# An attention and ternary feed-forward layer: weight sums totalled by a matmul with ones, the first split tiles of x in four buffers, order tables remade

## The chip, the core and the metric

The kernel runs on one core of a Trainium2 chip. The core has five engines with in-order queues of their own: TensorE (PE: matmuls and, beside them, weight loads), VectorE (DVE), ScalarE (ACT), GpSimd (POOL) and SyncE (SP), which here issues every DMA. They meet only at semaphores. The metric is the device time of one execution in microseconds (us), lower is better. A time is the median of several executions; the profile is of one execution.

## What is computed

```python
# 8 x 256 tokens, width 512; 16 heads of 32, 64 features a head; FFN width 2048
h  = layernorm(x)
q, k, v = h @ Wq.T + bq, ctx @ Wk.T + bk, ctx @ Wv.T + bv      # split into heads
qf, kf  = relu(q @ Wqf.T), relu(k @ Wkf.T) * mask
kv = sum_n kf v ; out = (qf kv) / (qf sum_n kf + 1e-8)
x  = x + out @ Wo.T + bo
# feed-forward with ternary weights and 8-bit activations
wq(w)  = clip(round(w / s), -1, 1) * s,   s = mean(|w|) over the whole matrix
xq     = 8-bit rounding of layernorm(x), row by row
a  = up(xq) * relu(gate(xq))**2 ; a = a * rsqrt(mean(a*a) + eps) * g
x  = x + down(8-bit rounding of a)
```

What matters below is s: the mean absolute value of each of the three matrices (gate, up, down). It is a sum over all rows and columns, so over all 128 partitions of the chip's memory too, and it must be known on every partition before a single weight can be rounded.

## The kernel before

There are two blocks. `attention` does everything up to the residual sum and makes the ternary weights on the side; `ffn` then runs over 16 tiles of 128 tokens. The change lies in the first alone.

**Turns.** The 16 token tiles are four groups of four. The attention block first makes keys and values of group 0 and then runs four turns, 0 to 3. Turn o does, for group o: F (key features), Q (queries), S (keys times values), R (query features), N (numerators and denominators); beside them K and V (keys and values) of group o+1 and O (output projection) of group o-1; turn 3 has P, the output projection of its own group. A unit such as Q2 fills one of the eight banks of PSUM, ACT reads the bank and writes the high half in fp16 (L747), DVE writes the low half (L879), and the bank is free. Each product is three fp16 matmuls (high by high, high by low, low by high). K, V, Q and O units are 12 matmuls of 128x512.

**What sets the order.** Nothing is scheduled at run time. `TURNS` is the order of the units on PE, and ACT and DVE go through the same list. `ACT_AFTER` and `DVE_AFTER` say behind which unit a piece of side work stands on those engines; POOL's and SP's orders are written out as lists of calls. A piece that stands too early blocks its engine until its input is there.

**Side work on the way to Q.** For tile n, `normalise` on ACT (L767) writes the normalised tile in fp32, into `xn` or, for tiles 1 and 2, into `o32`. `x_tile` on POOL splits it into two fp16 halves in `xn2` (L629, L632), which has two buffers; SP then issues a transposing DMA into `xT` (`turn_x`, L492). All Q units of a group wait for all four tiles. The attention's output goes the same way by `o_tile` (L641, L644), `o2` and `turn_o` (L501) to the O units. POOL also splits the context (L597 to L609, waits for `load_context`), adds the output bias (`add_bias`, L617) and makes the low half of kv (`kv_low`, L650).

**Side work on the weights.** Each of the three matrices comes in 8 pieces of 128x1024. `weigh(m, n)` on ACT sums the absolute values of a piece along each partition into a column of `wsum` (L795; its elementwise output goes to `junk`). `total(m)` on POOL sums the 8 columns over the partitions (L656). `weight_scale(m)` on DVE reduces the 8 totals to one number and inverts it into `winv` (L980 to L983). `chunk(c)` on ACT then rounds a piece with it (L807, through `wst`, two buffers) and takes the sign (L810). Matrix m is weighed in turn m and chunked in turn m+1. Pieces are loaded by SP (`raw_chunk`), some of them twice or three times, since space is scarce; `raw_up_even(k)` waits until the piece of gate weights in its place is rounded.

**Second layernorm.** DVE's `st2`, `large2`, `scale2` and `quant2` (L1186 to L1221) are statistics and 8-bit rounding of the group of the turn before.

Of the kernel before, what the change touches and what calls it, by code (L numbers as in the profile page):

```python
# [23 lines left out]
P = 128  # L24
# [32 lines left out]
def units(text):  # L57
# [9 lines left out]
    units(  # L67
# [4 lines left out]
    units(  # L72
# [4 lines left out]
    units(  # L77
# [19 lines left out]
        ("N", 6): (("weigh", 6),),
        ("K", 3): (("weigh", 7),),
# [41 lines left out]
    {  # L140
        ("F", 6): (("chunk", 0),),
        ("R", 4): (("kvh",),),
        ("R", 7): (("chunk", 1),),
        ("N", 1): (("chunk", 2),),
        ("N", 5): (("chunk", 3), ("chunk", 4)),
        ("O", 2): (("chunk", 5),),
# [7 lines left out]
        ("Q", 1): (("stats1",),),  # L154
        ("R", 3): (("ln1",),),
        ("N", 3): (("wo",),),
        ("V", 2): (("winv",),),
    },
    {
        ("F", 3): (("stats1",),),  # L160
        ("O", 0): (("st2", 0),),
        ("R", 3): (("st2", 1), ("ln1",)),
        ("Q", 3): (("st2", 2),),
        ("V", 0): (("st2", 3),),
        ("V", 1): (("large2",),),
        ("N", 7): (("scale2",),),
        ("V", 3): (("quant2", 0), ("quant2", 1), ("winv",)),
    },
    {
        ("O", 2): (("stats1",),),  # L170
        ("S", 0): (("st2", 1),),
        ("S", 1): (("ln1",),),
        ("R", 0): (("st2", 2),),
        ("K", 0): (("st2", 0),),
        ("N", 2): (("st2", 3),),
        ("N", 3): (("large2",),),
        ("V", 3): (("scale2",), ("quant2", 0), ("quant2", 1), ("winv",)),
# [3 lines left out]
        ("N", 3): (("st2", 1),),  # L181
        ("O", 3): (("st2", 3),),
# [15 lines left out]
    "O": "output projection",  # L198
}
# [79 lines left out]
def attention(nc, ps, xs, tern, area, ln2, wmean, x, ctxT, maskT, wqT, wkT, wvT, woT, wqfT, wkfT,  # L279
              bqT, bkT, bv, bo, wffn, xqb, xqT, xqb_ok, xqT_in):  # L280

    with ExitStack() as ctx:  # L282
# [45 lines left out]
        wtot = sb("wtot", [P, NCH])  # L328
# [89 lines left out]
        def _(sp):  # L418
# [1171 lines left out]
```

## Time and profile before

| | us |
|---|---|
| median of 3 executions | 445.12 (444.97 to 446.99) |
| profiled execution | 443.17 |
| its span, first to last instruction | 441.4 |
| attention block in it (until the barrier at 254.1) | 254.1 |
| PE busy in the span | 386.7 (88%) |
| DVE, ACT, POOL busy | 350.0, 316.9, 221.5 |

The profiled execution is 1.77 us longer than its span and 1.95 us shorter than the median. Times in the rows below are microseconds from the first instruction. "Idle before" is the time for which the engine did nothing ahead of the instruction, with the instruction that released it; "issue" stands where the profile shows no releaser.

### The profile page before, as it was taken

The page shows a single profiled execution, that of the slowest core. Times are in us where ns is not written, and L with a number is a line of the kernel's source. Part 1 is how long each engine was busy: PE and PEld are TensorE (multiplying, and loading weights), DVE is VectorE, ACT ScalarE, POOL GpSimd, SP SyncE. Part 2 cuts the span into 40 slices and gives each one's busy share as a digit, 9 for nine tenths or more (in the row PEclk, how much of TensorE's full clock was granted, in tenths as well). Part 3 has the DMA queues.
Part 4 walks back from the last instruction along what each step waited for, and adds up shares of the span by engine and source line. Part 5 has one row for each costly group of instructions (what it writes and reads, how often), then busy time and mean ns, then how long its engine had stood idle before and what let it go on. Part 6 is the DMA issues. An engine that isn't in the chain of part 4 may idle for free. (4 is left out here: it accounts for less than half of the span.)

```text
span 441.4 us, 8195 instructions
## 1 busy us (share of the span) xinstructions
PE 386.7 (88%) x2864; PEld 186.5 (42%) x2880; DVE 350.0 (79%) x718; ACT 316.9 (72%) x446; POOL 221.5 (50%) x210
## 2 busy tenths in 40 slices
PE   3986999819999889998979799899999989999955
PEld 1443545404555454455535344344444434344422
DVE  4765887472879589969888948999999999898962
ACT  5494387635978579888569359797979696988860
POOL 1074839162558428654276445474646463654420
PEclk9996999978999999999999989999999999999979
DMA  7846934736324904367064431452434242533324
GB/s 252 254 132 187 413 141 81 137 53 209 137 71 135 210 1 120 47 213 174 1 191 89 81 107 36 55 115 63 104 70 98 63 106 59 109 84 86 81 62 120
DMA packets 90872, 52.38 MB, mean 119 GB/s; under 512 B 78800, under 2 KB 78800, under 8 KB 90704
## 3 DMA queue, kind: packets, MB, share of 16 engines
q1 hardware_dynamic: 90832, 51.86, 45.5%
q8 instruction: 23, 0.38, 0.4%
q14 instruction: 17, 0.14, 0.1%
HBM read 28.78 MB, written 4.19 MB: 75 GB/s over the span
## 5 line engine op out<-in xcount | busy, mean ns | idle before, releaser
L1347 POOL TENSOR_TENSOR actg<-acts,subln 128x512 f32<-128x512 f32 x64 | 84.6, 1334 | 78.3 <-DVE acts L1430 73.8
L1527 PE MATMUL ps<-tern,area 128*128 128x512 bf16 x503 | 113.9, 382 | 3.8 <-PEq L282 2.7
L1527 PEld LDWEIGHTS ps<-tern,area 128*128 128x128 bf16 x512 | 49.8, 98 | 65.8 <-issue 4.9
L1540 PE MATMUL ps<-tern,aqT 128*128 128x512 bf16 x249 | 59.8, 390 | 12.3 <-DMA aqT<-aq 11.9
L1036 PE MATMUL ps<-xT,wqh 128*128 128x512 f16 x128 | 40.9, 403 | 13.4 <-DMA xT<-xn 13.4
L1358 ACT ACTIVATE relu<-ps 128x512 f32<-128x512 f32 x64 | 37.3, 582 | 21.2 <-PE ps L1527 21.2
L747 ACT ACTIVATE qkTh<-ps,bqk 128x512 f16<-128x512 f32 x32 | 21.4, 682 | 38.6 <-PE ps L1036 35.7
L1430 DVE TENSOR_TENSOR acts<-relu,ps 128x512 f32<-128x512 f32 x64 | 42.3, 679 | 5.9 <-ACT relu L1362 3.8
L1540 PEld LDWEIGHTS ps<-tern,aqT 128*128 128x128 bf16 x256 | 25.0, 100 | 45.6 <-DMA aqT<-aq 13.1
L1036 PE MATMUL ps<-woh,oT 128*128 128x512 f16 x128 | 40.1, 379 | 3.2 <-DVE vl L879 1.7
L879 DVE SCALAR_TENSOR_TENSOR fl<-ps,fh 128x512 f16<-128x512 f32 x64 | 40.3, 681 | 3.0 <-ACT fh L747 2.9
L879 DVE SCALAR_TENSOR_TENSOR qkTl<-ps,bqk,qkTh 128x512 f16<-128x512 f32 x32 | 23.5, 746 | 23.9 <-ACT qkTh L747 23.5
L1362 ACT ACTIVATE relu<-relu 128x512 f32<-128x512 f32 x64 | 40.3, 630 | 2.0
L1435 DVE TENSOR_REDUCE amax<-actg 128x1 f32<-128x1024 f32 x32 | 38.8, 1211 | 0.6 <-POOL actg L1347 0.2
L1369 ACT ACTIVATE square<-acts 128x2048 bf16<-128x2048 f32 x16 | 30.4, 1902 | 10.2 <-DVE acts L1430 10.2
L747 ACT ACTIVATE fh<-ps 128x512 f16<-128x512 f32 x64 | 34.2, 604 | 4.6 <-PE ps L1084 3.3
L1386 ACT ACTIVATE actg<-actg,magic_up,qs 128x2048 f32<-128x2048 f32 (+1 forms) x17 | 33.6, 1981 | 1.0 <-DVE qs L1449 1.0
L629 POOL TENSOR_TENSOR xn<-xn,zero 128x512 f16<-128x512 f32 x14 | 14.5, 1038 | 36.3 <-ACT xn L767 36.3
L641 POOL TENSOR_TENSOR o<-o,zero 128x512 f16<-128x512 f32 x16 | 16.6, 1036 | 30.4 <-issue 20.6
L1036 PE MATMUL ps<-ctxh,wkh 128*128 128x512 f16 x64 | 25.2, 394 | 7.3 <-DVE ctxl L867 7.3
L807 ACT ACTIVATE wst<-tern,magic,winv 128x1024 f32<-128x1024 f32 x20 | 24.7, 1234 | 8.9 <-issue 8.9
L1468 DVE TENSOR_SCALAR aq<-actg 128x2048 bf16<-128x2048 f32 (+1 forms) x17 | 23.8, 1401 | 7.9 <-ACT actg L1386 7.2
(160 smaller groups left out, 888.5 us busy)
## 6 DMA issues: line engine op xcount, KB each, us to landing
tern<-in_wffn SPq DMA_DIRECT2D x24, 512.0 KB, 5.4
out<-res SPq DMA_DIRECT2D x16, 256.0 KB, 2.1
area<-in_ctxT SPq DMA_DIRECT2D x3, 1024.0 KB, 5.5
xs<-in_x SPq DMA_DIRECT2D x3, 1024.0 KB, 10.0
oT<-in_wkT SPq DMA_DIRECT2D x4, 256.0 KB, 5.6
area<-in_ctxT SPq DMA_DIRECT2D x4, 256.0 KB, 6.1
fh<-in_wvT SPq DMA_DIRECT2D x4, 256.0 KB, 6.8
xs<-in_x SPq DMA_DIRECT2D x4, 256.0 KB, 7.5
```

The costliest lines, as they stand in the source:

```text
L747: nc.scalar.activation(out, in_, func, **kw).then_inc(high[stage], 1)
L879: nc.vector.scalar_tensor_tensor(out=out, in0=in0, scalar=scalar, in1=in1, op0=op0, op1=ALU.subtract).then_inc(drained[stage], 1)
L1036: mm = nc.tensor.matmul(acc, a, b, start=first and n == 0, stop=last and n == len(pairs) - 1)
L1347: nc.gpsimd.tensor_tensor(actg[:, s % 2, q], acts[:, s % 2, q], subln[:, q], ALU.mult)\
L1358: nc.scalar.activation(relu[:, u % 2, :], gate_bank(u), ACT.Relu).then_inc(relu_ok, 1)
L1362: nc.scalar.activation(relu2[:, u % R2, :], relu[:, u % 2, :], ACT.Square).then_inc(relu2_ok, 1)
L1369: nc.scalar.activation(square[:, :], acts[:, s % 2, :], ACT.Square, accum_out=ssq[:, s:s + 1])\
L1386: nc.scalar.activation(part, part, ACT.Identity, bias=magic_up[:, :], scale=qs[:, s:s + 1])\
L1430: nc.vector.tensor_tensor(acts[:, s % 2, 512 * c:512 * c + 512], relu2[:, u % R2, :], up_bank(u), ALU.mult).then_inc(acts_ok, 1)
L1435: return nc.vector.tensor_reduce(amax[:, s, h:h + 1], actg[:, s % 2, HALF * h:HALF * h + HALF], AX_X, ALU.max, apply_absolute_value=True)
L1527: mm = nc.tensor.matmul(acc, xqT[:, s % XT, k, :], weights[k][:, 512 * c:512 * c + 512], start=(k == 0), stop=(k == KC - 1))
L1540: mm = nc.tensor.matmul(down_bank(s), aqT[:, s % 2, k, :], down_w[:, k, :], start=(k == 0), stop=(k == FK - 1))
```

## The change

The sum over partitions leaves POOL. A new unit W is put into the list of turns 0 to 2, one for each matrix: PE multiplies a 128x128 fp32 matrix of ones by the 8 columns of `wsum`, so that each partition of a PSUM bank holds all 8 totals, and DVE reduces them from there. With that `total`, `wtot` and POOL's three reductions go.

`junk` becomes a view of the second buffer of `wst`; `chunk` uses only the first, and waits for the sign of the piece before. `split_x` puts the halves of tiles 2 and 3 into `o2`, the output's buffers, which are unused so early, so the first four tiles have four buffers; `o_tile` waits in turn until tiles 2 and 3 have been transposed.

The tables `TURNS`, `ACT_AFTER`, `DVE_AFTER` and the lists of POOL and SP are written anew. The diff, cut:

```diff
@@ TURNS, turn 1
-        "F0 F1 F2 F3 F4 F5 O0 O1 F6 F7 Q0 Q1 S0 S1 "
-        "O2 R0 R1 R2 R3 S2 S3 Q2 Q3 O3 K0 R4 R5 R6 "
-        "R7 K1 V0 N0 N1 N2 N3 V1 N4 N5 K2 N6 N7 V2 "
-        "K3 V3 "),
+        "F0 F1 F2 F3 O0 F4 F5 O1 F6 F7 S0 S1 Q0 Q1 "
+        "Q2 O2 R0 R1 R2 R3 K0 V0 Q3 S2 S3 K1 R4 R5 "
+        "R6 R7 O3 K2 V1 N0 N1 N2 N3 N4 N5 V2 K3 V3 "
+        "N6 N7 W0 "),
@@ DVE_AFTER, end of turn 2
-        ("V", 3): (("scale2",), ("quant2", 0), ("quant2", 1), ("winv",)),
+        ("N", 2): (("scale2",),),
+        ("N", 5): (("quant2", 0),),
+        ("K", 3): (("quant2", 1),),
@@ DVE_AFTER, end of turn 3
-        ("P", 0): (("st2", 2), ("large2",)),
-        ("P", 1): (("scale2",),),
-        ("P", 2): (("quant2", 0),),
-        ("P", 3): (("quant2", 1),),
+        ("P", 0): (("scale2",), ("quant2", 0)),
+        ("P", 1): (("quant2", 1),),
@@ buffers
-        junk = sb("junk", [P, CW], BF16)
+        ones = sb("ones", [P, P])
+        junk = wst[:, 1, :].bitcast(BF16)[:, 0:CW]
+        def split_x(n):
+            return o2[:, n % 2, :] if n in (2, 3) else xn2[:, n % 2, :]
@@ GpSimd
-                if n > 1:
+                if n > 3:
                     pool.wait_ge(xT_in[n % 2], landed(n - 2))
...
-            def total(m):
-                pool.wait_ge(weighed, (m + 1) * CPM)
-                own = slice(m * CPM, (m + 1) * CPM)
-                nc.gpsimd.partition_all_reduce(wtot[:, own], wsum[:, own], P, RADD).then_inc(tot_ok, 1)
@@ ScalarE, chunk
-                if c > 1:
-                    act.wait_ge(signed, c - 1)
+                if c > 0:
+                    act.wait_ge(signed, c)
@@ VectorE, weight_scale
-                dve.wait_ge(tot_ok, m + 1)
-                link(nc.vector.reduce_sum(wmean[:, m:m + 1], wtot[:, CPM * m:CPM * m + CPM], AX_X))
+                dve.wait_ge(filled["W"], m + 1)
+                link(nc.vector.reduce_sum(wmean[:, m:m + 1], ps[:, BANK["W", m, 0], 0:CPM], AX_X))
@@ TensorE
+                elif stage == "W":
+                    pe.wait_ge(weighed, (o + 1) * CPM)
+                    pe.wait_ge(magic_ok, 4)
+                    mm = nc.tensor.matmul(ps_bank[:, 0:CPM], ones[:, :], wsum[:, o * CPM:(o + 1) * CPM],
+                                          start=True, stop=True)
```

On POOL, around the first total (end of turn 0), there stands before, the split of x tile (1,2) first and that of (1,3) last:

```order
L629 TENSOR_TENSOR xn<-xn,zero 128x512
L632 TENSOR_TENSOR xn<-xn 128x512
L656 ISA
L656 ISA wtot<-wsum 128x8
L641 ISA
L641 TENSOR_TENSOR o<-o,zero 128x512
L644 TENSOR_TENSOR o<-o 128x512
L629 TENSOR_TENSOR xn<-xn,zero 128x512
L632 TENSOR_TENSOR xn<-xn 128x512
```

and in the changed kernel, between the same two splits:

```order
L633 TENSOR_TENSOR xn<-xn,zero 128x512
L635 TENSOR_TENSOR xn<-xn 128x512
L645 TENSOR_TENSOR o<-o,zero 128x512
L648 TENSOR_TENSOR o<-o 128x512
L645 TENSOR_TENSOR o<-o,zero 128x512
L648 TENSOR_TENSOR o<-o 128x512
L633 TENSOR_TENSOR xn<-xn,zero 128x512
L635 TENSOR_TENSOR xn<-xn 128x512
```

The reduction is gone, and with it the two ISA rows that carry no operands, one ahead of it and one behind.

On SP, from the last load of x for turn 2 to the fourth transpose of turn 1's x tiles, there stands before:

```order
L475 DMA xs<-in_x 128x4x512
L492 DMA_TRANSPOSE xT<-xn 128x8x128 x2
L501 DMA_TRANSPOSE oT<-o 128x8x128
L447 DMA tern<-in_wffn 128x1024 x2
L501 DMA_TRANSPOSE oT<-o 128x8x128
L492 DMA_TRANSPOSE xT<-xn 128x8x128
L501 DMA_TRANSPOSE oT<-o 128x8x128
L492 DMA_TRANSPOSE xT<-xn 128x8x128
L447 DMA tern<-in_wffn 128x1024 x2
L501 DMA_TRANSPOSE oT<-o 128x8x128
L481 DMA area<-in_ctxT 128x4x512 x2
```

and in the changed kernel:

```order
L480 DMA xs<-in_x 128x4x512
L497 DMA_TRANSPOSE xT<-xn 128x8x128
L486 DMA area<-in_ctxT 128x4x512
L452 DMA tern<-in_wffn 128x1024 x2
L497 DMA_TRANSPOSE xT<-xn 128x8x128
L506 DMA_TRANSPOSE oT<-o 128x8x128
L497 DMA_TRANSPOSE xT<-xn 128x8x128
L506 DMA_TRANSPOSE oT<-o 128x8x128 x2
L497 DMA_TRANSPOSE xT<-xn 128x8x128
L452 DMA tern<-in_wffn 128x1024
L506 DMA_TRANSPOSE oT<-o 128x8x128
```

The context of group 2 is loaded ahead of three of the four transposes instead of behind all of them.

On PE, at the end of turn 1, the W unit stands between the last N unit and the first F unit of turn 2:

```order
L1033 MATMUL ps<-kvh,fh 128x66
L1033 MATMUL ps<-kvl,fh 128x66
L1033 MATMUL ps<-kvh,fl 128x66
L1117 MATMUL ps<-wsum,ones 128x8
L1065 MATMUL ps<-feath,qkTh 128x2x64 x2
```

In turn 0 it stands between V2 and N6, in turn 2 between V3 and the first F unit of turn 3.

## Rows read from the trace of the kernel before

**Rows 1.** Busy time by stretch: turns 0 to 3, then the block's end.

```profile
core 0: us, PE busy (x) PEld busy (x) DVE busy (x) ACT busy (x) POOL busy (x), PEclk, DMA share, GB/s
30.17:79.45 49.28, 43.52 (x483) 23.51 (x482) 37.30 (x71) 31.48 (x54) 33.07 (x29) 0.93 0.61 200
79.45:145.40 65.95, 54.45 (x529) 27.96 (x528) 44.64 (x103) 44.45 (x63) 32.49 (x35) 0.92 0.49 120
146.94:202.60 55.66, 52.67 (x528) 27.52 (x528) 44.82 (x92) 43.71 (x63) 30.24 (x29) 1.00 0.47 121
204.21:251.80 47.59, 42.62 (x480) 22.85 (x480) 42.00 (x103) 32.92 (x44) 23.59 (x24) 1.00 0.40 94
```

**Rows 2.** PE's first matmuls behind its idle times, in order of time.

```profile
39.14 1.01 PE L1036 MATMUL ps<-xT,wqh 128*128 128x512 f16 x2 [3.62 <-DMA xT<-xn]
...
86.03 0.39 PE L1036 MATMUL ps<-woh,oT 128*128 128x512 f16 x1 [1.71 <-DVE vl L879]
...
99.37 1.01 PE L1036 MATMUL ps<-xT,wqh 128*128 128x512 f16 x2 [9.79 <-DMA xT<-xn]
...
157.56 0.23 PE L1068 MATMUL ps<-feath,qkTh 64*128 64x128 f16 x2 [1.23 <-issue]
...
204.21 0.23 PE L1068 MATMUL ps<-feath,qkTh 64*128 64x128 f16 x2 [1.42 <-DVE o L964]
...
226.78 0.42 PE L1084 MATMUL ps<-qkTh,feath 32*64 32x512 f16 x8 [1.43 <-DVE kvf L950]
```

**Rows 3.** POOL in order of time, around the first total.

```profile
77.15 1.16 POOL L632 TENSOR_TENSOR xn<-xn 128x512 f16<-128x512 f32 x1
84.32 0.43 POOL L656 PARTITION_ALL_REDUCE wtot<-wsum  x1 [6.01 <-issue]
91.61 1.03 POOL L641 TENSOR_TENSOR o<-o,zero 128x512 f16<-128x512 f32 x1 [6.86 <-issue]
...
94.95 1.15 POOL L632 TENSOR_TENSOR xn<-xn 128x512 f16<-128x512 f32 x1
```

**Rows 4.** Busy time by stretch: 9 matmuls behind the long wait; 24 elsewhere.

```profile
99.37:103.16 3.79, 3.79 (x9) 1.28 (x10) 0.00 (x0) 0.00 (x0) 0.48 (x1) 0.50 1.01 296
186.74:191.92 5.18, 5.18 (x26) 2.35 (x24) 3.58 (x7) 4.82 (x9) 3.84 (x3) 1.00 0.77 190
```

**Rows 5.** DVE and ACT where they wait for a total.

```profile
84.78 0.16 DVE L980 TENSOR_REDUCE wmean<-wtot 128x1 f32<-128x8 f32 x1 [6.29 <-POOL wtot L656]
...
156.32 0.16 DVE L980 TENSOR_REDUCE wmean<-wtot 128x1 f32<-128x8 f32 x1 [6.21 <-POOL wtot L656]
156.96 1.24 ACT L807 ACTIVATE wst<-tern,magic,winv 128x1024 f32<-128x1024 f32 x1 [6.43 <-issue]
```

**Rows 6.** POOL and DVE while the first x tiles are split.

```profile
29.18 1.04 POOL L629 TENSOR_TENSOR xn<-o,zero 128x512 f16<-128x512 f32 x1 [1.11 <-issue]
30.30 3.31 POOL L632 TENSOR_TENSOR xn<-o,xn 128x512 f16<-128x512 f32 x1
...
30.30 2.29 DVE L872 SCALAR_TENSOR_TENSOR wql<-wst,wqh 128x2048 f16<-128x2048 f32 x1 [1.05 <-ACT wqh L742]
```

**Rows 7.** Groups of instructions by line: mean ns of small matmuls and weighing.

```profile
L1036 PE MATMUL ps<-kvh,fh 128*128 128x66 f16 x128 | 12.7, 194 | 1.3 <-DVE fl L879 1.3
...
L795 ACT ACTIVATE junk<-tern 128x1024 bf16<-128x1024 f32 x24 | 25.2, 1051 | 0.6
```

**Rows 8.** DMA issues of the attention block: us from issue to landing.

```profile
tern<-in_wffn SPq DMA_DIRECT2D x24, 512.0 KB, 5.4
...
xT<-xn SPq DMA_TRANSPOSE x16, 3.1
```

**Rows 9.** DVE at the end of turn 2 and of the block; PE behind it.

```profile
207.72 1.92 DVE L1221 TENSOR_SCALAR xq<-xs,ln_means,ln_qscale 128x512 int8<-128x512 f32 x4
...
252.82 0.99 DVE L1221 TENSOR_SCALAR xq<-xs,ln_means,ln_qscale 128x512 int8<-128x512 f32 x2
...
254.52 15.78 PE L1527 MATMUL ps<-tern,area 128*128 128x512 bf16 x65 [2.67 <-PEq L282]
```

More of the change, by code:

```diff
@@ new lines @@
+        ("Q", 1): (("weigh", 1),),
+        ("O", 2): (("norm", 1),),
+        ("R", 0): (("chunk", 4),),
+        ("R", 1): (("norm", 2),),
+        ("K", 0): (("weigh", 2),),
+        ("S", 3): (("chunk", 5),),
+        ("O", 3): (("weigh", 3), ("kvh",), ("weigh", 4)),
+        ("N", 0): (("root2",),),
+        ("N", 1): (("chunk", 6),),
+        ("N", 2): (("chunk", 7),),
+        ("V", 2): (("weigh", 5), ("weigh", 6)),
+        ("V", 3): (("weigh", 7),),
+        ("W", 0): (("norm", 3),),
+    },
@@ new lines @@
+        ("Q", 3): (("chunk", 5),),
+        ("R", 7): (("norm", 2),),
+        ("K", 0): (("chunk", 6), ("chunk", 7)),
+        ("V", 1): (("root2",), ("norm", 3)),
+        ("N", 2): (("weigh", 2),),
+        ("N", 4): (("weigh", 3),),
+        ("N", 6): (("weigh", 4), ("weigh", 5)),
+        ("N", 7): (("weigh", 6),),
+        ("K", 3): (("weigh", 7),),
+    },
+    {
+        ("S", 1): (("chunk", 0),),
+        ("Q", 2): (("kvh",),),
+        ("O", 1): (("chunk", 1),),
+        ("N", 0): (("chunk", 2),),
+        ("N", 4): (("chunk", 3),),
+        ("N", 6): (("chunk", 4),),
+        ("N", 7): (("chunk", 5),),
@@ L153 @@
     {
[L154 to L157, printed above, removed]
-    },
-    {
[L160 to L167, printed above, removed]
-    },
-    {
[L170 to L176, printed above, removed]
-        ("V", 3): (("scale2",), ("quant2", 0), ("quant2", 1), ("winv",)),
+        ("R", 0): (("stats1",),),
+        ("K", 0): (("ln1",),),
+        ("N", 1): (("wo",),),
+    },
+    {
+        ("F", 0): (("stats1",),),
+        ("O", 1): (("st2", 0),),
+        ("S", 0): (("ln1",),),
+        ("R", 0): (("st2", 2),),
+        ("R", 1): (("st2", 1),),
+        ("O", 3): (("st2", 3), ("large2",)),
+        ("N", 3): (("scale2",),),
+        ("V", 2): (("quant2", 0),),
+        ("W", 0): (("quant2", 1),),
+    },
+    {
+        ("F", 2): (("stats1",),),
+        ("F", 4): (("st2", 1),),
+        ("F", 5): (("ln1",),),
+        ("S", 3): (("st2", 2),),
+        ("O", 3): (("st2", 3),),
+        ("R", 7): (("st2", 0),),
+        ("K", 0): (("large2",),),
+        ("N", 2): (("scale2",),),
+        ("N", 5): (("quant2", 0),),
+        ("K", 3): (("quant2", 1),),
     },
@@ L198 @@
     "O": "output projection",
+    "W": "total of a matrix's absolute raw weights, on all partitions",
 }
@@ L576, in _ @@
             nc.gpsimd.memset(zero[:, :], 0.0).then_inc(magic_ok, 1)
+            nc.gpsimd.memset(ones[:, :], 1.0).then_inc(magic_ok, 1)
             nc.gpsimd.memset(kvf[:, :, :, :], 0.0).then_inc(kv_zero, 1)
@@ L640, in o_tile @@
                     pool.wait_ge(oT_in[n % 2], landed(n - 2))
+                else:
+                    pool.wait_ge(xT_in[n % 2], landed(GT - 2 + n))
                 nc.gpsimd.tensor_tensor(o2[:, n % 2, 0:H], o32[:, n % 2, :], zero[:, :].broadcast_to((P, H)), ALU.add)\
@@ L664, in _ @@
             context_low(1)
+            mask_columns(1)
             add_bias(0, 0)
+            kv_low(0)
+            x_tile(1, 0)
             add_bias(0, 1)
             add_bias(0, 2)
[L668 to L669 removed]
             x_tile(1, 1)
[L671 removed]
             o_tile(0, 0)
+            x_tile(1, 2)
             o_tile(0, 1)
[L674 to L675 removed]
             o_tile(0, 2)
             x_tile(1, 3)
[L678 removed]
+            add_bias(0, 3)
             o_tile(0, 3)
@@ L683, in _ @@
             context_low(2)
+            x_tile(2, 0)
+            add_bias(1, 1)
+            x_tile(2, 1)
             kv_low(1)
-            mask_columns(2)
-            add_bias(1, 1)
-            x_tile(2, 0)
-            x_tile(2, 1)
+            x_tile(2, 2)
             o_tile(1, 0)
             o_tile(1, 1)
-            x_tile(2, 2)
-            o_tile(1, 2)
             add_bias(1, 2)
             x_tile(2, 3)
-            total(1)
+            o_tile(1, 2)
+            add_bias(1, 3)
+            mask_columns(2)
             o_tile(1, 3)
-            add_bias(1, 3)
             context_high(3)
@@ L790, in weigh @@
                 slot, uses = raw_place(m, SUM_ORDER[m][n])
+                if m == 0 and n == 0:
+                    act.wait_ge(w_low, 1)
                 act.wait_ge(raw_in[slot], 16 * uses)
@@ L993, in extra @@
                         first_ln(o + 1)
-                    if what == "winv":
-                        weight_scale(o)
                 if o > 0:
@@ L1053, in bank_free @@
                 before, group, index = BEFORE[stage, o, i]
-                pe.wait_ge(drained[before], group * PER[before] + index + 1)
+                pe.wait_ge(winv_ok if before == "W" else drained[before], group * PER[before] + index + 1)
             def key_features(o, t):
```

157 lines of the change are left out of this document (59 added, 98 removed), and 20 rows, old and new, of the table TURNS.

## The prediction

> **What bounds the kernel now.** I read the granted clock first, then the table by stretch, then PE's waits in order of time. The core is undisturbed, so the question is which engine each stretch hangs on. In the attention block [rows 1] PE is busy 43.5 of 49.3 us in turn 0, 54.5 of 66.0 in turn 1, 52.7 of 55.7 in turn 2 and 42.6 of 47.6 in turn 3; DVE reaches 44.8 of 55.7 in turn 2 and 42.0 of 47.6 in turn 3, ACT 43.7 and 32.9, POOL at most 33.1. So PE leads in turns 0 to 2, and turn 3 hangs on PE and DVE together. Turns 1 and 2 do the same kinds and number of units, yet turn 1 is 10.3 us longer. The reader is to see why in PE's waits [rows 2]: 9.79 us before the first Q matmul of turn 1, on a transposed x tile, and 1.71 just before. After the start all others are below 4 us.
>
> That wait leads back to POOL [rows 3]. The split of tile (1,2) ends at 78.31 (77.15 + 1.16). Then come 6.01 us in which POOL waits for nothing the profile shows, the all-reduce, recorded as 0.43, and 6.86 such us again: the next split starts at 91.61. So a total holds POOL for 13.30 us, of which 12.87 are no recorded work. In the order printed with the change an ISA row without operands stands exactly in each of the two gaps. The split of tile (1,3), the last that Q needs, ends at 96.10; its DMA lands about 3.1 us later [rows 8], and PE starts at 99.37. The other two totals hold POOL as long, but there PE has other units to do.
>
> The second half of the trace, from 254.1 on, is the feed-forward block. The change doesn't touch it, and it starts at a barrier; I carry it over at zero.
>
> **Part 1, the totals leave POOL.** Three times 13.3 us of POOL time go, 40 us; only what PE felt counts.
> Turn 1: without the total POOL would split output tile (0,2) from 78.3 on and tile (1,3) next, 2.2 us each by the two splits between 91.61 and 96.10 [rows 3], so done at 82.8 and landed at about 86. PE reached the Q units at 89.58 (99.37 - 9.79). The wait of 9.79 goes whole, with 3.6 us to spare. The clock goes with it: behind the wait 9 matmuls took 3.79 us at a granted clock of 0.50, that is 1.2 GHz, while 24 elsewhere (by the count of weight loads) took 5.18 at 1.00, that is 2.4 GHz [rows 4]; 9 of those cost 1.94, so 1.85 us come back. Together 11.6.
> DVE and ACT: DVE stood 6.29 and 6.21 us for the first two totals, ACT 6.43 for the second [rows 5], and behind DVE stood the low halves that free banks. PE felt that as 1.71 at 86.03 and 1.23 at 157.56 [rows 2]. Together 2.9, both gone if W is early enough (part 2).
>
> **Part 2, W comes to PE.** Three matmuls of 8 columns with 128x128 fp32 weights. No such operation is in the trace. From below: the small fp16 matmuls of 66 columns, 194 ns each by the record [rows 7] but overlapped, so a twelve-matmul unit N costs well under a microsecond; 0.05 us. From above: 1.01 us, what two matmuls of 512 columns with nothing ahead of them took at half clock [rows 2]. I take 0.3 each, nearer to the small rows since only 8 columns move: -0.9 in sum, ends -0.15 and -3.0. It cannot be a gain, as PE had no such work.
> The wait is the dearer item. W0 waits for the eighth weighing on ACT, and behind W0 stands all of PE's next turn. In turn 0 it is placed behind V1 and V2, two units of 2.6 us [rows 4], ahead of which the last weighing stands behind V1: V1's high half (512 columns, so less than the 1.05 of a weighing of 1,024 [rows 7]) and the weighing come to at most 2.1, under the 2.6 of V2. Nothing. In turn 2 V2 and V3 cover it in the same way. In turn 1 the cover is thin: the last piece may only be loaded when the eighth gate piece is rounded, which stands behind N2. From there ACT needs three operations of about 1.24 [rows 5], the load 5.4 to land [rows 8], the weighing 1.05 [rows 7]; that is 10.2, and up to 12 with what stands between, while PE needs N2 to N7, V2, K3 and V3, about 10. I charge 2.0 (ends 0 and 5).
> The three small DVE steps then read PSUM in place of SBUF; the cost is the same 0.16 us by nearest row [rows 5], and it is hidden beside PE's next units. The memset of ones lies in POOL's idle start. Both at nothing. The single `wst` buffer makes a rounding wait for the sign of the piece before; both run in order on ACT anyway, so it costs a semaphore's delay where two pieces stand together: nothing.
>
> **Here the Trainium skill speaks against the change.** The trace has the totals at 13.3 us of POOL each [rows 3]. The Trainium skill's page "GPSIMD Engine Reference", section 4.1 (Engine selection), gives a reduction along the partitions to GpSimd, and section 3.2 measures 247,699 ns for 2,048 columns. An estimate from that page is 121 ns a column, 1 us for 8 columns and 3 us for all three totals. By that the waits would come from elsewhere and the change would move next to nothing. That hangs on this rule and is the fourth rival. The recorded 0.43 us of the reduction itself doesn't contradict the page; the 12.87 around it do.
>
> **Part 3, four buffers for the first tiles.** The split of tile (0,2) waited 1.11 us for the transpose of (0,0); its second half then took 3.31 us where such a split takes 1.16, beside a two-input DVE operation of 2.29 that started in the same instant [rows 6]. With the wait gone this split is over before 30.30, but then tile (0,3) meets that DVE operation. So of 1.11 + 2.15 I take 1.0 (ends 0 and 2.3), taken off PE's 3.62 at 39.14 [rows 2].
>
> **Part 4, the tables.** Twelve-unit for twelve-unit the work is the same. What moves: the context of group 2 is asked for before the transposes rather than behind them, so POOL no longer waits for it in turn 1; the second layernorm's rounding of group 1 moves from the end of turn 2, where it cost DVE 1.92 us plus its scale at 207.72 [rows 9], into turn 2, where DVE has 10.8 us free [rows 1]. Turn 3 is where DVE counts, 42.0 of 47.6. PE's two named waits for DVE there are 1.42 and 1.43 [rows 2]; I take back 2.4 (ends 0 and 4.9, all that PE idles in turn 3 by [rows 1]). At the very end DVE rounds the last two tiles at 252.82 and ends at 253.81 [rows 9]; the rounding now stands a unit or more earlier, so the last residual sum sets the barrier: 0.9 (ends 0 and 1.0). Against it, new small waits of an order that is drawn tighter: 0.5.
> SP's queue: three load calls now stand ahead of transposes for turn 1, 2 MB in all. They were asked for 3 to 20 us before the transposes are needed, and the Q units have 3.6 us to spare plus two S units moved ahead of them. Nothing, unless a load's wait for `w_low` holds SP; `wo` on DVE stands two N units earlier than before.
>
> **The sum.** 11.6 + 2.9 - 0.9 - 2.0 + 1.0 + 2.4 + 0.9 - 0.5 = 15.4 us. The profiled execution of 443.17 would become 427.8, the span 426.0. The median lies 1.95 above the profiled execution, so 429.7.
>
> **Rivals.**
> 1. The forecast, 427 to 433: POOL's gaps were the cause and PE runs on.
> 2. DVE and ACT take over. At PE's pace turn 1 and turn 2 would take some 53 to 54 us, with DVE busy 44.8 and ACT 44.5 in each [rows 1]: 83%, and side work in order can leave either late at a bank. For it: turn 3, where DVE had 88%, left PE 5 us idle. Against: turn 2 ran in 55.7 with 6.2 us of DVE standing. If parts 3 and 4 give nothing and turns 1 and 2 each lose another 2: 445.1 - 11.6 - 2.9 + 0.9 + 2.0 + 4 = 437.5; between 433 and 440.
> 3. More than I count: all of PE's idle time in turns 0 and 3 is halved too (5.7 and 5.0 us [rows 1]) and W waits for nothing: 429.7 - 2.0 - 3.0 = 424.7; 421 to 427.
> 4. The reduction costs a microsecond and the gaps are something else on POOL that stays, or the code is fetched at another place all the same: gain 0 to 3, 442 to 445. Against it stand the ISA rows, of which none is left behind the first split.
> 5. Slower: W's wait. If the last up-weights come late in turn 1, because their load stands on SP behind a transpose that itself waits for a split on POOL, PE stands at W0 with the whole of turn 2 behind it and falls to half clock besides (1.85 us each time). It decides from 17.4 us of waiting in all, 5.8 in each of the three turns. At 8 a turn: 429.7 - 2 + 24 = 452.
>
> **Chances.** Rival 1 0.62, rival 2 0.21, rival 3 0.11, rival 4 0.03, rival 5 0.03. The likeliest gives the time, 429.7. The range leaves out rivals 4 and 5, the upper end of rival 2 and the lower of rival 3: 423.5 to 436.5. This kernel can be told from no change at about 0.5%, 2.2 us. Faster by more: rivals 1 to 3 and part of 4, 0.95; within: 0.03; slower: 0.02.
>
> **What would show it.** Right: no gap of 6 us on POOL; no wait over 3 us before the first Q of turn 1 and the clock at 1.00 there; turn 1 at 53 to 57 us; the barrier at about 239. Wrong: PE waiting at the W matmul for more than 3 us in turn 1 (part 2); PE waits for DVE or ACT adding up to over 5 us in turns 1 and 2 (rival 2); turn 3 still over 47 us (part 4); a clock below 0.9 in turn 1 from a new idle time.

## The result, and the profile after

| | before | after |
|---|---|---|
| median of 4 executions, us | 446.06 (444.97 to 451.21) | 427.00 (425.13 to 431.09) |
| profiled execution, us | 443.17 | 425.52 |
| its span | 441.4 | 423.7 |
| mean granted clock of PE | 0.969 | 0.980 |
| first matmul of the feed-forward block | 254.52 | 237.29 |
| PE, DVE, ACT, POOL busy | 386.7, 350.0, 316.9, 221.5 | 386.0, 354.2, 317.7, 220.7 |

The ratio is 0.956, with a 95% interval of 0.946 to 0.967: faster. The work of each engine is what it was; only the waits went. First the busy time by stretch in the changed kernel, turns 0 to 3 (the columns are those of [rows 1]):

```profile
29.95:79.22 49.27, 44.82 (x483) 24.29 (x483) 37.43 (x74) 32.03 (x55) 32.26 (x30) 0.93 0.75 234
79.22:133.50 54.28, 52.62 (x528) 27.57 (x528) 47.47 (x99) 46.28 (x68) 30.77 (x29) 1.00 0.53 136
134.55:188.60 54.05, 52.39 (x528) 27.67 (x529) 49.23 (x110) 46.26 (x66) 33.57 (x33) 1.00 0.50 114
189.16:234.60 45.44, 42.16 (x480) 22.98 (x480) 40.38 (x90) 31.29 (x39) 23.37 (x23) 1.00 0.43 100
```

In these stretches turn 1 went from 65.95 us at a clock of 0.92 to 54.28 at 1.00. In the profiled executions turn 1 starts 0.2 us earlier (79.22 for 79.45). Counted from one turn's first F matmul to the next, turn 1 is shorter by 12.2 (67.49 to 55.33), turn 2 by 2.7 (57.27 to 54.61), and turn 3 with the block's tail, up to the barrier (254.1 and 237.0), by 2.0; the feed-forward block is 0.6 shorter. That is 17.7 us.

PE of the changed kernel, in order of time (start, duration, instruction; in brackets the idle time before it and its releaser):

```profile
34.48 0.23 PE L1065 MATMUL ps<-feath,qkTh 64*128 64x128 f16 x2 [3.02 <-DVE vl L876]
...
38.03 0.58 PE L1033 MATMUL ps<-xT,wqh 128*128 128x512 f16 x1 [0.77 <-DMA xT<-o]
...
75.33 0.29 PE L1117 MATMUL ps<-wsum,ones 128*128 128x8 f32 x2
75.47 0.19 PE L1033 MATMUL ps<-kvh,fh 128*128 128x66 f16 x1
...
89.77 0.59 PE L1033 MATMUL ps<-xT,wqh 128*128 128x512 f16 x2
...
133.54 0.36 PE L1117 MATMUL ps<-wsum,ones 128*128 128x8 f32 x2 [1.18 <-issue]
134.55 0.23 PE L1065 MATMUL ps<-feath,qkTh 64*128 64x128 f16 x2 [0.65 <-DVE qkTl L876]
...
188.63 0.28 PE L1117 MATMUL ps<-wsum,ones 128*128 128x8 f32 x2
```

Against [rows 2]: Q of turn 1 starts at 89.77 with no wait, where it started at 99.37 after 9.79. The three W units cost 0.14 (75.33 to 75.47), 0.36 and 0.28; one of them waits, 1.18. POOL in the same place as [rows 3], from the end of the split of tile (1,2) on:

```profile
74.91 1.16 POOL L635 TENSOR_TENSOR xn<-xn 128x512 f16<-128x512 f32 x1
76.03 1.04 POOL L645 TENSOR_TENSOR o<-o,zero 128x512 f16<-128x512 f32 x1
...
79.38 1.15 POOL L648 TENSOR_TENSOR o<-o 128x512 f16<-128x512 f32 x1
...
81.61 1.16 POOL L635 TENSOR_TENSOR xn<-xn 128x512 f16<-128x512 f32 x1
```

No gap is left, and the split of tile (1,3) ends at 82.77 (81.61 + 1.16), where it ended at 96.10. At the block's start, the place of [rows 6], the slow pair has only moved by one tile: POOL's second half at 31.65 now takes 3.08, DVE's two-input operation at 30.56 takes 3.16 rather than 2.29, and PE waits 3.02 for DVE there (1.67 before).

### The profile page after: what moved, and what is told of

The parts are those of the page before. It is cut to its first block and busy times, and to the rows that moved or that the text cites. A ratio compares the mean times of both kernels' runs of the same rounds, so it can differ in the third digit from the quotient of the medians.

```text
span 423.7 us, 8200 instructions
## 1 busy us (share of the span) xinstructions
PE 386.0 (91%) x2870; PEld 187.9 (44%) x2886; DVE 354.2 (84%) x718; ACT 317.7 (75%) x446; POOL 220.7 (52%) x208
## 5 line engine op out<-in xcount | busy, mean ns | idle before, releaser
L1529 PE MATMUL ps<-tern,area 128*128 128x512 bf16 x503 | 112.5, 379 | 3.7 <-PEq L283 2.7
L1542 PE MATMUL ps<-tern,aqT 128*128 128x512 bf16 x249 | 61.5, 398 | 11.6 <-DMA aqT<-aq 11.1
L1033 PE MATMUL ps<-xT,wqh 128*128 128x512 f16 x128 | 39.5, 391 | 0.8 <-DMA xT<-o 0.8
L807 ACT ACTIVATE tern<-wst,magic 128x1024 bf16<-128x1024 f32 x24 | 27.6, 1149 | 0.8
```

Source lines behind the costliest of these rows:

```text
L1033: mm = nc.tensor.matmul(acc, a, b, start=first and n == 0, stop=last and n == len(pairs) - 1)
L1529: mm = nc.tensor.matmul(acc, xqT[:, s % XT, k, :], weights[k][:, 512 * c:512 * c + 512], start=(k == 0), stop=(k == KC - 1))
L1542: mm = nc.tensor.matmul(down_bank(s), aqT[:, s % 2, k, :], down_w[:, k, :], start=(k == 0), stop=(k == FK - 1))
```

## The experiments

The experiments ran on three chips; each kernel below was compared with the kernel before on its own chip, so what is compared across chips is the ratio to that. In the traces turns 1 to 3 are compared by their lengths, not by their place in the span: turn 0 alone took from 45.95 to 51.25 us in the kernels below, while turn 1 took 55.31 to 55.34 in all six that have the new tables and no total on POOL.

**Whose are the gaps: the reduction's?** The kernel before with the all-reduce replaced by a copy on POOL, order and tables untouched. This kernel leaves out the sum over the partitions: each partition goes on with its own sum.

```diff
-                nc.gpsimd.partition_all_reduce(wtot[:, own], wsum[:, own], P, RADD).then_inc(tot_ok, 1)
+                nc.gpsimd.tensor_copy(wtot[:, own], wsum[:, own]).then_inc(tot_ok, 1)
```

> The kernel before with POOL's all-reduce replaced by a copy of the 8 columns, so that each partition uses its own sum: the sum over the partitions is left out, all else stands. Theory: the two 6 us gaps around each total go with the reduction, 430 to 433, within 1.5 of the matmul version with old tables. Rival (the gaps are something else on POOL at these places): gaps stay, 442 to 445. Rival (W on PE is dear): this is 3 or more below the matmul version.

Measured: 428.81 us, ratio 0.961 (0.954 to 0.968). POOL where [rows 3] had its gaps:

```profile
78.53 1.16 POOL L632 TENSOR_TENSOR xn<-xn 128x512 f16<-128x512 f32 x1
79.64 0.19 POOL L656 COPY wtot<-wsum 128x8 f32<-128x8 f32 x1
79.78 1.04 POOL L641 TENSOR_TENSOR o<-o,zero 128x512 f16<-128x512 f32 x1
```

Both gaps go with the reduction, and with them nearly all that the change gains: 0.961 here, 0.956 there. But it is gained at other places: turn 1 takes 53.6 us here and 55.3 in the changed kernel, turn 3 with its tail 52.9 and 48.1. DVE of this kernel, at the end of turn 2, is wanted further down:

```profile
191.55 5.09 DVE L1221 TENSOR_SCALAR xq<-xs,ln_means,ln_qscale 128x512 int8<-128x512 f32 x4
```

**Is it the reduction's work, or getting to it?** The kernel before with each reduction done twice in a row.

```diff
+                nc.gpsimd.partition_all_reduce(wtot[:, own], wsum[:, own], P, RADD).then_inc(tot_once, 1)
+                pool.wait_ge(tot_once, m + 1)
                 nc.gpsimd.partition_all_reduce(wtot[:, own], wsum[:, own], P, RADD).then_inc(tot_ok, 1)
```

> The kernel before with each all-reduce made twice in a row. Theory (the gaps are the exchange of POOL's code, once ahead of and once behind the reduction): the second follows the first within 1.5 us, and a total holds POOL 14 to 15 us in place of 13.3. Rival (each reduction itself takes the 13 us, whatever the profile records): a second gap of 6 or more between the two, and a hold of 20 to 27 us.

Measured: 445.91 us in one execution (the kernel before: 443.87 on this chip). POOL around the first pair:

```profile
85.82 0.43 POOL L656 PARTITION_ALL_REDUCE wtot<-wsum  x1 [5.98 <-issue]
86.34 0.40 POOL L658 PARTITION_ALL_REDUCE wtot<-wsum  x1
93.82 1.03 POOL L641 TENSOR_TENSOR o<-o,zero 128x512 f16<-128x512 f32 x1 [7.08 <-issue]
```

The second reduction adds 0.52 us (86.34 - 85.82). The 5.98 ahead and the 7.08 behind are there once each, for two reductions as for one. They belong to the switch from POOL's elementwise operations to the reduction and back; what POOL does in them the traces don't show. The third total of the kernel before tells more of the way back:

```profile
210.96 0.41 POOL L586 COPY vh<-maskh 128x32 f16<-128x32 f16 x1
...
218.28 1.03 POOL L641 TENSOR_TENSOR o<-o,zero 128x512 f16<-128x512 f32 x1 [6.76 <-issue]
```

Two copies of mask columns run right behind that reduction with no gap, and the 6.76 us come behind them, ahead of the first TENSOR_TENSOR. So not every operation other than the reduction pays for the way back.

The Trainium skill, page "GPSIMD Engine Reference", section 2.1 (Instruction dispatch), says that the first call of a freshly loaded GpSimd kernel pays about 6 us (5.95 measured) for its code, with no instruction in the profile. The trace agrees in size, 5.98, and shows more than that: a gap of that kind stands at all three totals and not only at the first, and another on the way back. Whether it is the loading of code, no run here shows. The estimate that the prediction took from section 3.2 of that page, 1 us a total, is over twice the recorded work of 0.43 and leaves out what surrounds it.

**Is it the split behind the total that PE waited for?** The kernel before with the first total moved behind the split of tile (1,3); nothing else.

```diff
-            total(0)
             o_tile(0, 2)
             x_tile(1, 3)
+            total(0)
```

> The kernel before with the first total moved behind the split of tile (1,3) on POOL, and nothing else. Theory: the 9.8 us wait and its slow clock go, but the total comes about 4.5 us later, and DVE and ACT, which stand at it in order, hold PE's banks: PE waits 5 to 7 there instead of 1.7, so 437 to 440. Rival (only the place of the total mattered): 432 to 434.

Measured: 438.17 us, ratio 0.984 (0.978 to 0.989).

```profile
90.83 0.61 PE L1036 MATMUL ps<-woh,oT 128*128 128x512 f16 x1 [5.96 <-DVE vl L879]
```

The wait of 9.79 is gone, and this one, 1.71 in [rows 2], has grown to 5.96: DVE now waits 10.54 us for the total where it waited 6.29, with the low half of V ahead of PE's O unit queued behind. Seven of the 18 us can be had by a swap of lines; for the rest the total must leave POOL.

**Four buffers alone.** The kernel before with `split_x`, the wait for `n > 3` and the wait of `o_tile` that belongs to them.

> The kernel before with tiles 2 and 3 split into the output's buffers, and nothing else. Theory: POOL no longer waits 1.1 us, the split of tile (0,3) meets the two-input DVE operation instead, Q of turn 0 starts about 1 us earlier (38.0 in place of 39.1), and the gain is lost again in part since that DVE operation takes about 0.9 longer. Rival: no change at all, 39.1.

Measured: 442.5 us in one execution (443.87 before on this chip). POOL, DVE and PE:

```profile
31.37 3.08 POOL L636 TENSOR_TENSOR o<-xn,o 128x512 f16<-128x512 f32 x1
...
30.30 3.14 DVE L878 SCALAR_TENSOR_TENSOR wql<-wst,wqh 128x2048 f16<-128x2048 f32 x1 [1.05 <-ACT wqh L748]
...
37.75 1.01 PE L1042 MATMUL ps<-xT,wqh 128*128 128x512 f16 x2 [0.76 <-DMA xT<-o]
```

Q starts 1.4 us earlier than in [rows 2], and the wait of 1.11 that POOL had is gone; the slow second half of a split stays. Whether time is gained isn't shown: turn 0 took 48.97 to 51.25 us in the five other kernels with two buffers (49.28 in the kernel before) and 45.95 to 50.31 in the eight with four (48.67 here).

**Totals on PE with the old tables.** W stands behind F3 of the next turn, where no wait is left ahead of it.

```diff
-        "F0 F1 F2 F3 F4 F5 O0 O1 F6 F7 Q0 Q1 S0 S1 "
+        "F0 F1 F2 F3 W0 F4 F5 O0 O1 F6 F7 Q0 Q1 S0 S1 "
...
-            total(0)
```

> The kernel before with the totals made by the ones matmul (with the single rounding buffer that makes room for it) and every table and list left as it was; W stands behind F3 of the next turn, the scale on DVE with it. Theory (POOL's hold is the cause): the wait before turn 1's Q goes with its slow clock, 11.6 us, and the 2.9 us behind DVE and ACT; W costs under 1: 431 to 433, and in the trace no POOL gap of 6 us. Rival (the new order of the tables brings most of the gain): 437 or more, with PE still waiting over 4 us before turn 1's Q.

Measured: 436.76 us, ratio 0.981 (0.977 to 0.985), near the rival's 437, though without the rival's wait: nothing over 1.02 us stands ahead of turn 1's Q. It is also 8 us above the kernel with the copy, where 3 or more was to be the sign that W on PE is dear. W itself isn't: its two matmuls are recorded with 0.39 us, with no wait ahead. Turn 1 takes 57.0 us here and 53.6 there, turn 2 54.2 and 53.7, turn 3 with its tail 56.2 and 52.9. In turn 1 it is PE's waits for DVE, 1.02 and 3.01 for 1.33; they aren't traced further. Against the kernel before, turn 3 with its tail takes 56.2 us (191.00 to 247.18) where it took 50.3 before (204.21 to 254.52). PE's wait there, and behind it DVE and POOL of the same kernel:

```profile
202.25 0.61 PE L1030 MATMUL ps<-xT,wqh 128*128 128x512 f16 x1 [5.51 <-DVE fl L873]
...
192.62 0.17 DVE L1227 RECIPROCAL ln_rstd<-ln_sd 128x4 f32<-128x4 f32 x1
192.82 0.90 DVE L1228 TENSOR_TENSOR ln_t<-ln_rstd 128x4 f32<-128x4 f32 x1
193.76 1.19 DVE L1229 TENSOR_TENSOR ln_t<-ln_t,ln_var 128x4 f32<-128x4 f32 x1
194.99 0.97 DVE L1230 TENSOR_SCALAR ln_t<-ln_t 128x4 f32<-128x4 f32 x1
...
192.55 1.16 POOL L645 TENSOR_TENSOR o<-o 128x512 f16<-128x512 f32 x1
193.67 1.27 POOL L618 TENSOR_TENSOR xs<-xs,bob 128x512 f32<-128x512 f32 x1
194.90 1.04 POOL L642 TENSOR_TENSOR o<-o,zero 128x512 f16<-128x512 f32 x1
```

These are DVE operations on 4 numbers a partition. Each of the slow ones ends when POOL's operation ends: 193.72 and 193.71, 194.95 and 194.94, 195.96 and 195.94. The same ten operations before:

```profile
206.04 0.16 DVE L1229 TENSOR_TENSOR ln_t<-ln_rstd 128x4 f32<-128x4 f32 x1
...
206.43 0.17 DVE L1231 TENSOR_SCALAR ln_t<-ln_t 128x4 f32<-128x4 f32 x1
...
210.66 0.43 POOL L656 PARTITION_ALL_REDUCE wtot<-wsum  x1 [6.27 <-issue]
```

Before, scale and rounding took DVE 3.8 us (205.84 to 209.64), all of it inside POOL's 6.27 us gap. In this kernel the same work took 9.0 (192.62 to 201.59). So a second theory: DVE's operations of certain kinds stand still while POOL runs one, and the reduction's gaps had kept POOL out of their way. The kernel before shows it too, one turn earlier, where a split ran on POOL until 148.92: the four roundings took 2.75 us, not 1.92.

```profile
147.37 2.75 DVE L1221 TENSOR_SCALAR xq<-xs,ln_means,ln_qscale 128x512 int8<-128x512 f32 x4
```

**The rounding put back.** The changed kernel with the scale and rounding of group 1 again at the end of turn 2.

```diff
-        ("N", 2): (("scale2",),),
-        ("N", 5): (("quant2", 0),),
-        ("K", 3): (("quant2", 1),),
+        ("V", 3): (("scale2",), ("quant2", 0), ("quant2", 1)),
```

> The changed kernel with the second layernorm's scale and rounding of group 1 put back to the end of turn 2 on DVE. Theory: 3.8 us of DVE work fall on the start of turn 3, where DVE and PE are level: 1.5 to 3 slower than the changed kernel. Rival (DVE is not on the path there): within 0.5.

Measured: 433.74 us, ratio 0.977 (0.973 to 0.981), where the changed kernel has 0.959 on another chip: 7 to 8 us lost where 1.5 to 3 were expected. By the traces it is 8.3: turns 1 to 3 with the tail take 166.4 us (77.10 to 243.47), and 158.1 in the changed kernel (79.22 to 237.29).

```profile
189.34 1.04 DVE L1213 TENSOR_SCALAR ln_ends<-ln_ends 128x4 f32<-128x4 f32 x1
...
190.63 0.97 DVE L1215 SCALAR_TENSOR_TENSOR ln_qscale<-ln_qscale,ln_rstd 128x4 f32<-128x4 f32 x1
191.64 3.90 DVE L1221 TENSOR_SCALAR xq<-xs,ln_means,ln_qscale 128x512 int8<-128x512 f32 x4
...
196.06 0.28 PE L1063 MATMUL ps<-feath,qkTh 64*128 64x128 f16 x2 [5.11 <-DVE winv L978]
```

The four roundings take 3.90 where [rows 9] has 1.92, and the kernel without a reduction 5.09. PE waits 5.11, and from 196.06 to 199.00 the granted clock is 0.50, that is 1.2 GHz.

At its new place, in the changed kernel, the rounding is no faster:

```profile
185.11 2.09 DVE L1223 TENSOR_SCALAR xq<-xs,ln_means,ln_qscale 128x512 int8<-128x512 f32 x2
...
188.93 1.86 DVE L1223 TENSOR_SCALAR xq<-xs,ln_means,ln_qscale 128x512 int8<-128x512 f32 x2
```

That is 3.95 for the four. The move doesn't keep DVE and POOL apart; it puts the slow rounding where PE waits little for it, 0.74 at 183.44 and 0.24 at the start of turn 3.

**The second theory, put to the test.** That kernel with one wait more: POOL may not go on until DVE has rounded group 1.

```diff
             add_bias(2, 2)
+            pool.wait_ge(quantised, 4)
             o_tile(2, 3)
```

> The changed kernel with the rounding of group 1 back at the end of turn 2 (as in the run before, 433.7 us), and one wait more: GpSimd does its last split and its last bias sum of that stretch only when VectorE has rounded group 1. Nothing is left out. Theory, that VectorE's operations on SBUF stand still while a GpSimd operation runs: with GpSimd standing, the small scale operations cost 0.16 to 0.18 us each without exception, the four roundings 1.9 in sum rather than 3.90, VectorE is through with both about 3.5 us earlier, PE's wait of 5.11 at the start of turn 3 falls to 1.5 to 2, and the kernel takes 430 to 431 us although GpSimd is given a wait. Rival, that the order of VectorE's work alone costs the time: the roundings stay at 3.5 or more, the wait at 5, and the time at 433.7 or above it, by what GpSimd's delay of about 3 us costs.

Measured: 427.58 us, ratio 0.959 (0.956 to 0.963), level with the changed kernel on the same chip (below), and better than the 430 to 431 expected.

```profile
191.60 0.16 DVE L1216 SCALAR_TENSOR_TENSOR ln_qscale<-ln_qscale,ln_rstd 128x4 f32<-128x4 f32 x1
191.80 1.91 DVE L1222 TENSOR_SCALAR xq<-xs,ln_means,ln_qscale 128x512 int8<-128x512 f32 x4
...
193.79 1.04 POOL L643 TENSOR_TENSOR o<-o,zero 128x512 f16<-128x512 f32 x1 [4.13 <-DVE xq L1222]
...
194.23 0.23 PE L1064 MATMUL ps<-feath,qkTh 64*128 64x128 f16 x2 [1.42 <-DVE winv L979]
```

POOL does nothing for 4.13 us, and turns 1 to 3 with the tail take 158.2 us (79.78 to 238.00) in place of 166.4; by the ratios it is 7 to 8 us. DVE's operations are at 0.16 to 0.18 and 1.91 again, PE's wait is 1.42, and the clock from 194.23 to 197.00 stays at 1.00. A wait added to POOL gave back all that the late rounding had cost. This theory stands.

The Trainium skill, page "SBUF — State Buffer", section "Who interferes with whom", names a mechanism that would do this: VectorE and GpSimd share a pair of SBUF ports as an exclusive lock, taken for a whole instruction; VectorE wants it for two SBUF inputs and in the two-port modes that `tensor_scalar` can enter, and not otherwise. The rows agree: TENSOR_TENSOR and TENSOR_SCALAR stand until POOL's end, RECIPROCAL at 192.62 beside POOL takes 0.17, and the low halves, which read one input from PSUM, take 0.68 to 0.75 beside POOL. That it is the ports and nothing else that the two engines share, no run here isolates.

**New tables without the freed POOL.** The changed kernel with the totals back on POOL, ahead of the same output tiles as in the kernel before, and DVE's scale at the end of each turn; no W on PE.

> The changed kernel with the totals back on POOL, one ahead of the split of output tile (0,2), (1,3) and (2,2), no W on PE, the scale on DVE at the end of each turn; new tables otherwise. Theory: tile (1,3) comes 13 us later again, PE waits 8 to 10 before turn 1's Q and runs 2 us at half clock, and DVE waits for the totals: 439 to 444. Rival (the tables bring most): 434 or less.

Measured: 461.47 us, ratio 1.039 (1.032 to 1.045). That is 17 us beyond the upper end of the expectation. PE:

```profile
99.22 0.58 PE L1042 MATMUL ps<-xT,wqh 128*128 128x512 f16 x1 [7.05 <-DMA xT<-xn]
...
160.14 0.23 PE L1074 MATMUL ps<-feath,qkTh 64*128 64x128 f16 x2 [4.11 <-DVE fl L885]
...
229.31 0.21 PE L1042 MATMUL ps<-vh,fh 128*128 128x65 f16 x1 [9.38 <-POOL vl L592]
```

The new order is drawn so tight that each total is felt: the first by Q, the second by way of DVE, which stands 9.03 us for it, the last by PE's S units of turn 3, which need the masked columns that POOL writes behind it. With the totals on POOL these tables are a loss of 16 us, so they are no gain of their own; they are an order for a free POOL.

**The old tables with the rounding moved.** Totals on PE, old order; scale and rounding of group 1 into the N units of turn 2 (with the steps ahead of them, ACT's root too, some units earlier), and DVE's statistics of turn 1 behind W's scale rather than ahead of it.

```diff
-        ("V", 3): (("scale2",), ("quant2", 0), ("quant2", 1)),
+        ("N", 3): (("scale2",),),
+        ("K", 3): (("quant2", 0),),
+        ("N", 6): (("quant2", 1),),
```

> The tables of before with the totals on TensorE (436.8 us in the earlier run), in which two things are moved: scale and rounding of group 1 from behind V3 of turn 2 into its N units (the steps ahead of them two units earlier, too), and VectorE's first statistics of turn 1 behind F4 rather than ahead of W's total. Nothing is left out. Theory: the waits of 5.51 at the start of turn 3 and of some 3 to 5 on ScalarE in turn 1 were most of what separates this kernel from the changed one; with them gone 431 to 433 us, 4 to 6 less than before the move. Rival: the remaining rows of the tables do it (the order of Q, S and O units, the transposes and loads on SP); then 435 or more.

Measured: 437.77 us, ratio 0.982 (0.979 to 0.986): no gain, where 431 to 433 us were expected.

```profile
192.28 1.04 DVE L1233 TENSOR_TENSOR ln_rstd<-ln_rstd,ln_t 128x4 f32<-128x4 f32 x1
...
192.27 1.04 POOL L632 TENSOR_TENSOR xn<-xn,zero 128x512 f16<-128x512 f32 x1
...
198.00 0.29 PE L1064 MATMUL ps<-feath,qkTh 64*128 64x128 f16 x2 [7.50 <-DVE o L960]
```

The scale met POOL in its new place as well: POOL splits an output tile as soon as DVE's division has made it, and right behind the division stands the scale. DVE spent 5.3 us on the ten operations (189.78 to 195.05), the divisions behind them came late, and PE waited 7.50 at the start of turn 3, where before the move it waited 5.51 a little later. ACT's wait for W's scale fell from 4.85 to 1.10 us, and turn 1 from 57.0 to 55.7; turn 2 took 61.6 for 54.2, turn 3 with its tail 51.9 for 56.2. In the changed kernel three of these ten operations, from 178.39 on, are held by 2.1 us in all, and PE's one wait behind them is the 0.74. Which other rows of the new tables make that possible isn't settled.

**Can the wait at W be saved?** Two ways: the total of turn 1 behind F3 of turn 2, and, in a second kernel, the eighth weighing of turn 1 ahead of V3's high half on ACT.

```diff
@@ the first kernel
-        "N6 N7 W0 "),
+        "N6 N7 "),
...
-        "F0 F1 F2 F3 O0 O1 F4 F5 F6 F7 Q0 S0 S1 Q1 "
+        "F0 F1 F2 F3 X0 O0 O1 F4 F5 F6 F7 Q0 S0 S1 Q1 "
@@ the second kernel
-        ("V", 3): (("weigh", 7),),
+        ("K", 3): (("weigh", 7),),
```

> The changed kernel with the second W moved from the end of turn 1 to behind F3 of turn 2. Theory: PE's 1.2 us at W and part of the 0.9 and 0.7 behind it go: 1 to 2 us less than the changed kernel, 425 to 426. Rival: the bank and DVE's chain behind W take as much there: no change.

> The changed kernel with the eighth weighing of turn 1 ahead of V3's high half on ScalarE instead of behind it. Nothing is left out. In the changed kernel the W matmul of turn 1 waits 1.18 us for that weighing, and the first matmul of turn 2 then another 0.65 for VectorE's low half of K3, which ends at 134.40. Theory of the prediction's part 2, that the wait at W is paid in full: 1.0 to 1.2 us less than the changed kernel on the same chip. Rival: the first F unit waits for that low half whether W waits or not, so the wait at W covers itself; W then comes at about 132.4 with no wait, F at 134.5 as before, and the time is the same within 0.3 us.

> The changed kernel itself, beside the other three on this chip, as the base of their comparison. Both theories expect the ratio of the first measurement, 0.957, within 0.01: 424 to 428 us.

Measured: the first 429.06 us, ratio 0.967 (0.962 to 0.972), not faster than the changed kernel and rather slower, with a new wait of PE for DVE of 1.91 us at 155.16; the second 426.68, ratio 0.958 (0.954 to 0.962); the changed kernel beside it 427.22, ratio 0.959 (0.956 to 0.963). PE at the start of turn 2, first kernel, then second:

```profile
134.35 0.23 PE L1066 MATMUL ps<-feath,qkTh 64*128 64x128 f16 x2 [2.18 <-DVE qkTl L877]
```

```profile
132.05 0.36 PE L1117 MATMUL ps<-wsum,ones 128*128 128x8 f32 x2
134.36 0.29 PE L1065 MATMUL ps<-feath,qkTh 64*128 64x128 f16 x2 [1.94 <-DVE qkTl L876]
```

With W elsewhere or unhindered, turn 2 starts at 134.35 and 134.36, and in the changed kernel at 134.55; turn 1 takes 55.31, 55.34 and 55.33 us. The first F unit waits for DVE's low half of K3 whatever W does: the 1.18 at W lay under another wait. In the second kernel the single idle stretch of 1.94 us was followed by 2.64 us at a granted clock of 0.50 (134.36 to 137.00), where the changed kernel, whose idle time W broke in two, kept 1.00, as did the first kernel behind its 2.18. What tells these cases apart stays open.

## Why the prediction was right, step by step

- **POOL's gaps and the Q units, 11.6.** Right, mechanism and size. Turn 1 is 12.2 us shorter; the prediction's parts for it (11.6 + 1.7, less W's wait and its matmul) come to 11.0. Tile (1,3) was foreseen as split at 82.8 and was at 82.77. The second reduction at 0.52 us shows that the 13.3 us were the switch and not the reduction's work.
- **DVE and ACT standing for totals, 2.9.** The waits of 1.71 and 1.23 are gone. In their stead PE has 0.51 at 80.58, and 0.92 two units into turn 2, so part of this was not gained. These two alone are more than the 0.5 booked for "new small waits"; what made up for them was that small waits of before went as well, which the sum didn't count (see the sum below).
- **The W matmuls, 0.9.** Measured 0.14, 0.36 and 0.28, so 0.8 for the three: right.
- **The wait at W, 2.0.** The cover was thin as foreseen, 1.18 us. But the step was booked on the wrong engine: DVE's low half ends at 134.40 and holds the next F unit regardless, so W's own price is nothing: turn 1 has the same length with W elsewhere or with no wait ahead of it. What the turn's start costs (1.18 + 0.36 + 0.65) is DVE's.
- **Four buffers, 1.0.** Q of turn 0 starts 1.1 us earlier (38.03 for 39.14), and 1.4 in the kernel with that alone. The price was named too (DVE's operation met by the next tile); it went from 2.29 to 3.16, and PE's wait there from 1.67 to 3.02. But the gain didn't last: from 38.03 to 42.00 the granted clock is 0.51, so the earlier units ran at half speed, and by the first F of turn 1 only 0.2 is left. Given how much turn 0 varies, no gain from this part is shown.
- **Turn 3 and the tail, 2.4 + 0.9.** The step that failed, though its number nearly held, by luck: turn 3 with the tail gained 2.0. The argument was that moving the rounding frees DVE of the 1.92 us of [rows 9]. But 1.92 was the price beside a POOL that stood in its gap, and this gap the change removes. At its old place the rounding would have cost 3.90 in the new kernel and 5.09 in the one without a reduction, and PE 5.11 us plus half clock: 8 us of time. At its new place it takes 3.95, but PE waits only 0.74 and 0.24 us behind it. So the move did not free DVE of 1.92; it kept PE clear of a loss of 8 that the prediction did not see coming. [rows 6] had shown the same collision, 3.31 beside 2.29, and it was read there as a matter of one tile. A reading was off too: the named wait of 1.42 stands ahead of turn 3's first matmul, so it is no part of the 4.9 us that PE idles in turn 3. It fell to 0.24, which counts for turn 2 here, and the wait of 1.43 to 1.04.
- **Sum.** 15.4 forecast, 17.7 in the profiled executions. By stretch (turn 3 and the tail at 3.3 less the 0.5 for new waits) the surplus is 1.2 in turn 1, 1.8 in turn 2 and 0.6 in the feed-forward block, and 0.8 is short in turn 3 and 0.5 in turn 0. The 1.8 of turn 2 are small waits: before, PE waited 1.23, 0.35, 0.54, 0.49, 0.38 and, at the turn's end, 1.42 us, 4.4 in all, of which the sum took back only the 1.23; in the changed kernel it waits 0.92, 0.74 and 0.24, 1.9 in all. The signs held: turn 1 at 54.3 us and a clock of 1.00, the barrier at 237.0.
- **Rival 2,** DVE and ACT take over: the waits of PE in turns 1 and 2 add up to 4.2 with the one at W, most of it DVE's or ACT's, and the sign was 5. It came near, and in the kernels with old tables it did come (436.8 and 437.8).
- **Rival 3,** more than counted: the median of 427.0 lies on the border between it and the forecast. PE's idle time fell from 5.8 to 4.5 in turn 0 and from 5.0 to 3.3 in turn 3, not by half, and W cost nothing but its matmuls. Its sum was off as well: half of 5.7 and 5.0 is 5.35, which is 1.95 and not 3.0 above the 1.0 and 2.4 already booked.
- **Rival 4,** the gaps are something else: refuted by the copy (0.961) and the doubled reduction.

## What to carry to other kernels

A short cross-partition reduction on GpSimd is dear for what surrounds it (13 us around 0.4 of work), and a matmul with ones does it in 0.1 to 0.4 us if its input is ready and something covers the wait. Before an idle stretch of one engine is removed, look at which operations of another engine lie in it: their durations are those of an undisturbed engine and may not carry over. Where VectorE's two-input or rounding operations on SBUF stand on the critical path, holding GpSimd back for them can be worth more than keeping it busy.

## What the runs showed of the hardware

- The switch to the reduction cost POOL 5.79 to 7.81 us and the way back 6.70 to 7.47, at all three totals in each of the five kernels that had them; a second reduction in a row 0.52. Copies of 128x32 right behind a reduction ran without a gap; the gap came ahead of the first TENSOR_TENSOR.
- A DVE operation on 128x4 elements took 0.16 us alone and up to 1.20 beside POOL, ending with POOL's; four roundings of 128x512 took 1.91 to 1.92 alone, 2.75 to 5.09 beside POOL.
- A POOL wait of 4.13 us at the right place made the kernel 7 to 8 us faster.
- Idle times of PE of 5.11 and 5.51 us were followed by a granted clock of 0.50 for at least 2.7 us. One of 1.94 was too (2.6 us), while 2.18 and 1.42 elsewhere, and the pair 1.18 and 0.65, were not. One of 3.01 was followed by 0.50 (the kernel with the total behind the split, at 143.46) and one of 3.01 by 1.00 (totals on PE with the old tables, at 136.83). The length of the last idle time alone doesn't decide it.
